# Node stages of a four-layer graph network: the table's bias through TensorE and the table's copy on ScalarE

## Time and profile before

| what | us |
|---|---|
| three runs | 8808.49, 8825.83, 8867.62 |
| their median | 8825.83 |
| the profiled execution's own time | 8858.47 |
| its span | 8856.7 |
| mean granted TensorE clock | 0.839 of 2.4 GHz |
| node stage 0 | about 2196 to 2325 of the span |
| node stage 1 | about 4440 to 4600 |
| node stage 2 | about 6640 to 6730 |

### The profile page before, as it was taken

How to read it: one execution, slowest core, us unless ns; L and a number is a source line. 1 busy time by engine, 2 the same in 40 slices (tenths; PEclk the granted TensorE clock), 3 DMA queues, 4 the chain that set the end, 5 groups by cost and what they waited for, 6 DMA issues and landing times.

```text
span 8856.7 us, 139305 instructions
## 1 busy us (share of the span) xinstructions
PE 6966.1 (79%) x41611; PEld 5845.8 (66%) x41612; DVE 5009.7 (57%) x12625; ACT 2082.7 (24%) x7255; POOL 6268.2 (71%) x6594
## 2 busy tenths in 40 slices
PE   6999999999777777777767777777775777777775
PEld 4777777777566666666656666666664666666664
DVE  3333333334766666666676666666657666666666
ACT  2222222222422222222232222222222222222222
POOL 4777767776677777777747777777765777777774
PEclk7989988999887887887858888888887888888887
DMA  3323322332222222222222222222222222222221
GB/s 97 78 74 79 80 71 75 80 78 72 76 67 66 66 67 67 67 66 67 64 79 69 69 69 69 69 69 69 69 62 74 69 69 69 69 69 69 69 70 50
DMA packets 425473, 625.68 MB, mean 71 GB/s; under 512 B 189634, under 2 KB 305617, under 8 KB 425293
## 3 DMA queue, kind: packets, MB, share of 16 engines
q0 software_dynamic: 206336, 462.61, 21.5%
q1 hardware_dynamic: 219086, 162.49, 7.1%
HBM read 598.03 MB, written 26.58 MB: 71 GB/s over the span
## 4 chain that ended last, share of the span: by engine, by line
PE 42%; POOL 23%; issue 15%; DVE 12%; DVEq 4%; DMA 2%; SPq 1%; ACT 1%; POOLq 0%; ACTq 0%
POOL G L561 22%; PE ps L707 12%; PE ps L754 8%; PE ps L729 8%; PE ps L724 7%; DVEq L1216 3%; PE ps L697 3%; DVE msg L1335 2%; DVE acc L1242 2%; DMA G<-rows,idx 1%; PE ps L775 1%; DVE acc L1232 1%; DVE shared L1289 1%; DVE shared L1297 1%; PE ps L785 1%
## 5 line engine op out<-in xcount | busy, mean ns | idle before, releaser
L561 POOL DMA_INDIRECT G<-rows,idx x6448 | 6126.8, 950 | 2219.4 <-issue 1907.7
L1162 DVE TENSOR_TENSOR memb<-rel,ps 128x1664 f32<-128x1664 f32 x496 | 936.4, 1888 | 1861.6 <-PE ps L707 1861.3
L707 PE MATMUL ps<-msg,memb 128*128 128x136 f32 (+2 forms) x12896 | 1755.3, 297 | 125.4 <-DVE msg L1335 123.6
L707 PEld LDWEIGHTS ps<-msg,memb 128*128 128x128 f32 x12896 | 1677.1, 205 | 153.7 <-issue 77.5
L754 PE MATMUL ps<-membT,shared 128*104 128x128 f32 x9672 | 1728.7, 350 | 2.2 <-ACT membT L919 2.2
L754 PEld LDWEIGHTS ps<-membT,shared 128*104 128x104 f32 x9672 | 1560.8, 230 | 25.8 <-issue 3.0
L697 PE MATMUL ps<-ident,memb 128*128 128x128 f32 x6448 | 1081.7, 309 | 467.8 <-DVE memb L1162 425.7
L1242 DVE TENSOR_TENSOR acc<-acc,ps 128x136 f32 (+2 forms) x3472 | 1023.0, 295 | 425.6 <-DVE acc L1242 346.1
L697 PEld LDWEIGHTS ps<-ident,memb 128*128 128x128 f32 x6448 | 786.3, 154 | 686.1 <-issue 363.9
L919 ACT ACTIVATE membT<-ps 128x512 f32<-128x512 f32 x1984 | 954.2, 505 | 74.9 <-PE ps L697 63.6
L1335 DVE TENSOR_TENSOR msg<-G,ps 128x1768 f32<-128x1768 f32 x372 | 742.6, 1996 | 197.3 <-PE ps L785 193.9
(11 more groups left out here) (180 smaller groups left out, 4621.3 us busy)
## 6 DMA issues: line engine op xcount, KB each, us to landing
G<-rows,idx POOLq DMA_INDIRECT x6448
shared<-marks_all SPq DMA_DIRECT2D x372, 156.0 KB
shared<-in_edge_attr SPq DMA_DIRECT2D x124, 256.0 KB
shared<-in_edge_attr SPq DMA_DIRECT2D x124, 160.0 KB
rows<-msg SPq DMA_DIRECT2D x36, 288.0 KB, 2.8
idx<-in_src SPq DMA_DIRECT2D x496, 6.5 KB
xrows<-msg SPq DMA_DIRECT2D x24, 256.0 KB, 2.2
memb<-xrows SPq DMA_DIRECT2D x24, 256.0 KB, 3.1
```

Source lines behind the costliest of these rows:

```text
L561: nc.gpsimd.indirect_dma_start(G[:, b, t, 0:rows[l].shape[1]], None, rows[l], bass.IndirectOffsetOnAxis(idx[:, b, t:t + 1], 0)).then_inc(g ...
L707: last = mm(ps_sum[k // 2][:, 0:width], memb[:, b, k * P:(k + 1) * P], msg[:, b, k, 0:width], start=k % 2 == 0, stop=k % 2 == 1 or k == K - 1)
L1162: tt(memb[:, b, :].rearrange("p (k n) -> p k n", k=K), r, w, ALU.is_equal).then_inc(memb_ready, 1)
```

## The change

`table` and its two calls go from VectorE. On PE, `table_products` begins with a product of one row of ones with the one-row bias for each bank (304 columns, 152 for the last block), which stands ahead of the wait for `n_kept` and behind the wait for `n_tab_in`; the four products then add to it. On ACT, `keep_scores` becomes `keep_table`: it waits as `table` did, copies the block (608 columns from two banks) to SBUF in one instruction, signals `n_tab_in` and goes on with the copies of the scores as before. For l = 2 the table leaves PSUM in slot s+3 now, not in slot s+2.

```diff
             def table_products(l, s):
                 g = NS * l + s
-                pe.wait_ge(n_kept, g + 1)
                 if s:
                     pe.wait_ge(n_tab_in, g)
+                for h in range(-(-QN[s] // 2)):
+                    m = min(2, QN[s] - 2 * h)
+                    mm(n_tab[h][:, 0:m * RW].rearrange("p (q n) -> p q n", q=m), ones[0:1, :],
+                       biasrep[0:1, l, :].unsqueeze(1).to_broadcast([1, m, RW]), start=True, stop=False)
+                pe.wait_ge(n_kept, g + 1)
                 for q in range(QN[s]):
                     n = s * BLK + q * P
                     last = mm(n_tab[q // 2][:, (q % 2) * RW:(q % 2 + 1) * RW], xT[:, n:n + P], wext[:, l, :],
-                              start=True, stop=True)
+                              start=False, stop=q % 2 == 1 or q == QN[s] - 1)
                 last.then_inc(n_tab_out, 1)
...
-            def keep_scores(l, s):
+            def keep_table(l, s):
 
                 g = NS * l + s
-                n = QN[s]
+                n, r = QN[s], g % 2
+                if g >= 2:
+                    act.wait_ge(stored[r], 16 * ring_uses(g, 2))
+                    act.wait_ge(n_adt, g - 1)
+                act.wait_ge(n_tab_out, g + 1)
+                h = -(-n // 2)
+                w = n // h * RW
+                copy(tab[:, r, 0:n, :].rearrange("p (h q) n -> p h (q n)", h=h),
+                     ps[:, 4:4 + h, 0:w]).then_inc(n_tab_in, 1)
                 act.wait_ge(n_tab_in, g + 1)
...
-            def table(l, s):
-                g = NS * l + s
-                n, r = QN[s], g % 2
-                if g >= 2:
-                    dve.wait_ge(stored[r], 16 * ring_uses(g, 2))
-                    dve.wait_ge(n_adt, g - 1)
-                dve.wait_ge(n_tab_out, g + 1)
-                for h in range(-(-n // 2)):
-                    m = min(2, n - 2 * h)
-                    o = tt(tab[:, r, 2 * h:2 * h + m, :], n_tab[h][:, 0:m * RW].rearrange("p (q n) -> p q n", q=m),
-                           biasrep[:, l, :].unsqueeze(1).to_broadcast([P, m, RW]), ALU.add)
-                o.then_inc(n_tab_in, 1)
...
-                        s = at(t, 3)
-                        if s is not None:
-                            table(l, s)
...
-                        s = at(t, 2)
-                        if s is not None:
-                            table(l, s)
```

More of the change, by code:

```diff
@@ L1077, in node_stage @@
                     if s is not None:
-                        keep_scores(l, s)
+                        keep_table(l, s)
                     s = at(t, -2)
```

## The result

The forecast was 8876 us, within 1%. The kernel after takes 8933.35 us, the median of 6 runs (8918.25 to 8946.84), against 8832.86 for 6 runs of the kernel before (8808.49 to 8867.62): a ratio of 1.0108 with a 95% interval of 1.0094 to 1.0123, so 83 to 109 us. The sign was right. The size was half of what came, the time lies above the range, which ended at 8925, and "slower by over 1%", which came, had a chance of 0.11.

The account below looks back on a forecast made before the run. The chain of waits was PE 42%, GpSimd 23%, VectorE 12%, mostly in unchanged edge stages. Removal 0, stage 2 +25, stage 1 +15, stage 0 +10 made +50: 8908.5 us as profiled, 8876 at the median; range 8828 to 8925.

Parts of the forecast that it names:

- The removal, 0 us: Node stages: taking 75 additions off VectorE gains nothing in steady slots; bounds 0 and -31.5 us.
- the shadow: Stages 0 and 2: VectorE's additions lie beside its wait for GpSimd's power, with some 0.3 us idle left after them.
- the rival by which it would come earlier: GpSimd's power comes earlier without VectorE's additions beside it; at most 31.5 us less, 8794 us; chance 0.05.
- The ring in stage 2: `outer`, copy, bias, table, turn, `keep_rows` close once per slot: 8.5 us against 5.73 at 1.2 GHz; +25 us.
- +15 forecast: Stage 1: PE has no free time, slots grow from 9.11 to at most 11.3 us; +1.4 over 11 slots.
- +10 forecast: Stage 0: slots of 8.53 us lengthen by a middle +0.9 over 11 slots.
- The forecast's ring: Stage 0: hidden products, `keep_hidden`, `outer`, copy, bias and table close in 8.7 us against a slot of 8.53.
- 2 us more in a slot with the table at the low clock: Stage 0: a slot whose table products run at the low clock takes 2 us more than 8.7.
- The rival in which the clock falls in stage 0: Longer waits pause PE, stage 0's granted clock nears 0.6, slots reach 12.9 us; +103 us, 8929; chance 0.1.
- The rule weighed: PE kept busy stays at full clock, so added products pay for themselves and stage 1 loses nothing; trace agreed only partly.
- The rival that was built on a rising clock: More PE work makes all three node stages hold 2.4 GHz; +4 us, 8830; chance 0.2.
- the second rival: PE's clock falls in stage 0 too, through pauses waiting for the copy; +103 us, 8929; chance 0.1.

Follow-up runs that it names:

- before again: The kernel before, unchanged, profiled once more on the chip with edge stages of 2.0 to 2.1 ms: 8839.89 us.
- after again: The kernel after, unchanged, profiled once more on the chip with edge stages of 2.0 to 2.1 ms: 8907.17 us.
- bias products alone: Kernel after, but VectorE copies the table out of PSUM where it used to add, ScalarE as before: 8852.05 us, 1.0021 of the kernel before.
- bias twice: Kernel after with each one-row bias product made twice, the second overwriting the first: 8998.01 us, 1.0185 of the kernel before.
- early copy: Kernel after with ScalarE's table copy first in its slot, ahead of `inner` and `outer`: 8895.10 us, 1.0053 of the kernel before.
- turn first: Kernel after with PE's turn ahead of the bias and table products of its slot: 8887.35 us, 1.0047 of the kernel before.
- the last version: Kernel before, stage 2 only: early ScalarE table copy, no bias product or VectorE addition, later block's sums in VectorE's wait: ratios 0.9983, 0.9986, 0.9990.

## Why the prediction was right in sign and wrong in size

The forecast's sum failed in three places. It counted 11 slots per stage at the price of a steady one and the filling and the end at nothing; these slots carry 26 of the 79 us. It took the hidden products of stage 0 at the high level of the clock (3.37 us to their end), where they take 5.06. And it took the edge stages as they were, where edge stage 1 is 13 to 14 us longer. Its three terms for the steady slots add up to 50, and 52 were measured, but that is luck in part: stage 0's was too small (10 for 17), and the other two a little too large (15 for 12, 25 for 23).

**The sums agree with the marks.** For each kernel, the change of its node stages, plus 13 where the rhythm is in turns (the distance of the edge stage 1 in the pair before again and after again), beside the measured ratio:

| | stages | with edge 1 | by the ratio |
|---|---|---|---|
| after | +79 | +92 | +83 to +109 |
| bias products alone | +29 | +29 | +4 to +34 |
| bias twice | +149 | +162 | +142 to +185 |
| early copy | +38 | +51 | +28 to +65 |
| turn first | +38 | +51 | +22 to +61 |

**The removal, 0 us: right.** The 1.05 to 1.12 us of waiting for the power stand where 1.1 was forecast. That the shadow can be filled, with 13 us of gain, fits it from the other side. No run took the additions away alone, but with VectorE idle beside it GpSimd's power still takes 1.01 us, so the rival by which it would come earlier with them gone is out.

**The costs of the parts: right.** The copy 0.66 (0.68 forecast), the bias pair 1.22 and 2.32 (1.2 and 2.2), the table as before. One step of the working was off, without weight: 1.12 times 304/512 is 0.67, not "0.6 us or less"; by the measured pair a product is 0.61.

**The ring in stage 2: the mechanism right, the term too small.** +25 forecast, +31 measured. The ring at the low level is 8.5 by forecast and 8.49 by measurement. The middle value of 2.3 was near, too: the third to the eleventh slot take 74.5 us against 51.5, 2.55 each, or 23 in all. What was missing is outside them: the second slot, in which the ring first closes, went from 5.76 to 10.74, and the last from 2.10 to 5.14, together 8 us. Two different cuts open the ring (the turn first, the copy on VectorE), and a third shortens it by just the link it takes out, so the ring is shown.

**Stage 1: the slot right, the ends left out.** +15 forecast, +21 measured. The slot of 10.03 is inside 9.1 to 11.3. The nine middle slots carry 12 us (8.75 on average before and 10.08 after), about my +1.4 each. The slots at the ends, which I left out, carry another 8.4: the first went from 11.23 to 13.15, the last two from 5.79 and 3.30 to 8.87 and 6.70. Of the kernels with the copy on ScalarE at its old place, PE bounds the stage only when the turn goes first; as it stands the ring of stage 1 bounds it, with 1.06 us of waiting per slot.

**Stage 0: the term that failed most.** +10 forecast, +27 measured. The nine middle slots carry 17.4 of it (75.5 to 92.9 us, 1.93 each for the 0.9 forecast), and the ends 9.2 (the first slot from 9.54 to 12.69, the last two from 4.49 and 3.29 to 8.87 and 5.00). The forecast's ring was 3.37 + 0.67 + 1.65 + 0.70 + 1.2 + 1.1 = 8.7. The slot after is 5.06 (2234.11 to 2239.17, the end of L819) + 0.62 + 1.54 + 0.71 + 1.22 + 1.13 = 10.28. The hidden products account for +1.69, and the rest comes out 0.1 lower. I had taken their 3.37 from a slot at 1.00 and assumed that it would stay, though each turn of the ring has a pause of PE in it (0.93 us ahead of the bias). The rule of "2 us more in a slot with the table at the low clock" looked at the wrong products: the table and the bias run at the high level here, and the hidden products fell. The rival in which the clock falls in stage 0 gave a time (8929) close to the measured one, but its mechanism didn't come: it wanted slots of 12.9 us with PE full near 0.6, and the stage has 0.74, with PE waiting in each slot.

**Edge stages as they were: wrong, by 11 to 14 us in one of four.** I had said that a difference from there would make me wrong. About one seventh of it comes from there.

**The rule weighed.** The forecast held against it that a busy slot of stage 1 stood at the low level. The runs go further: with the turn first, PE had no pause in eight slots of stage 1 and was granted 0.50 in them. The Trainium skill, page "TensorE: Matmul & The Clock Gate", section "Why this matters for your kernels", promises the full clock to an engine kept busy. For these short fp32 products the runs don't bear it out, and the measurement decides. The rival that was built on a rising clock is out.

**The range** was too narrow above. It allowed 8903 for the low level everywhere and took only part of the second rival, while nothing in it stood for the 26 us of the stage ends or the 13 to 14 of edge stage 1.

What stays open: what sets the rhythm of edge stage 1. With 25 tiny instructions more on VectorE ahead of it the old one came back, but only one profile shows it, and whether by the program's length or by something else that they shift wasn't told apart. How the old and the new rhythm lead to stages that differ by 11 us, although two chunks last 34.10 and 34.13, was not followed. What lets the clock fall in front of the hidden products of stage 0 is also only seen together with the ring: both cuts of the ring that were tried there on PE's and ScalarE's side (turn first, early copy) brought the mean of L814 from 1038 ns back to 704 and 754, but none held the pause fixed and changed the rest.

## What to carry to other kernels

Before moving an operation to an engine with room, follow each signal it gives to the next instruction in line on both engines, and on until you are back at the start: if the chain closes, its length and not anyone's busy time is the new slot. Work that lies beside a longer wait is free to do and worth nothing to remove, until something else fills the wait. Price such a ring at the level of the clock that the ring itself will leave (work after each stop, not the row of a slot that ran through), and count all blocks of a short loop, its start and end too: with 13 blocks they were a third of the loss here.

## What the runs showed that I had not expected

- Edge stage 1 can run in two rhythms, 17.05 us for each chunk or 18.74 and 15.39 in turns. The one in turns has the higher mean granted clock (0.84 to 0.85 against 0.80 to 0.81) and the longer stage, 2134 to 2135 against 2118 to 2128.
- A GpSimd power of 128x4 takes 1.01 us when VectorE stands idle or adds from PSUM beside it, and 1.41 when VectorE adds 64x544 elements between SBUF tiles beside it. The gain of the last version is net of this. The Trainium skill, page "SBUF — State Buffer", section "SBUF: two separate sides", states that a VectorE operation with two inputs in SBUF and a GpSimd operation that reads SBUF take their common ports in turns, the later one blocked. The longer record agrees with that in its direction. But the next VectorE addition of the same kind (L1409, 0.72 us beside the rest of the power) isn't longer than the first (0.71), and no run here took the sums apart to test the rule.
- TensorE was granted 0.50 for eight slots of 11.18 us without a pause, and 0.60 and 0.62 on average for the same products in two other kernels.
- A chip on which the edge stages take 3.0 ms instead of 2.05, with the node stages the same within 2 us or so. In its traces VectorE waits where the other chip's doesn't (some 1680 us in edge stage 1, against 815), but what for wasn't found.
